# Splitting the row maxima and applying the first norm on GpSimd, and a router chain of one step per slot, in a fused memory, attention and expert kernel

## The reference, cut to what matters

```python
z = layernorm(x)                       # "the first norm" of this text
q, k, v = z @ Wq + bq, z @ Wk + bk, z @ Wv + bv
probs = softmax(einsum("bqhd,bkhd->bhqk", q, k) / sqrt(8))
attn = einsum("bhqk,bkhd->bqhd", probs, v) @ Wo + bo
x2 = layer_norm(z + attn) * ln1_g + ln1_b
keys = x2 @ router_w + router_b
expert = floor(keys) mod 4
out = x + layer_norm(x2 + expert_ffn[expert](x2)) * ln2_g + ln2_b
```

## Time and profile before

| | |
|---|---|
| median of 3 runs | 1465.96 us (1462.61 to 1480.37) |
| the profiled execution | 1456.27 us, span 1454.5 us |
| busy over the span | PE 1163.3 us (80%), DVE 1035.3 (71%), ACT 790.5 (54%), POOL 490.2 (34%) |
| maxima reduced on VectorE, L1287 | 1024 times, 643.0 us busy |
| exponentials on ScalarE, L1012 | 1024 times, 548.5 us busy |
| mean granted TensorE clock | 0.889 of full speed |

### The profile page before, as it was taken

The page is one execution under the profiler, slowest core; times in us unless marked ns, Lnnn a source line. Parts: engine busy times, 40 slices in busy tenths (PEclk is TensorE's granted clock), DMA queues, the critical chain, the costliest instruction groups (busy, mean ns, idle before and its releaser), DMA issues. The chain is left out here.

```text
span 1454.5 us, 24976 instructions
## 1 busy us (share of the span) xinstructions
PE 1163.3 (80%) x6087; PEld 464.3 (32%) x6087; DVE 1035.3 (71%) x2549; ACT 790.5 (54%) x1638; POOL 490.2 (34%) x579
## 2 busy tenths in 40 slices
PE   4978894479889889889889889889889850887872
PEld 4754452112223323323323323323322210333331
DVE  7357772578889889889989889889889321355553
ACT  2323331027677677677767678678677740443431
POOL 6323333011043143143143243243242231245453
PEclk9998875559899999999989899899999985999996
DMA  5000000422332332332331431431431004344340
GB/s 140 3 1 0 0 0 0 87 66 49 64 82 46 83 82 44 83 82 44 82 82 37 89 82 34 92 82 32 94 81 25 16 15 149 116 122 139 111 145 6
DMA packets 101868, 94.12 MB, mean 65 GB/s; under 512 B 23101, under 2 KB 93182, under 8 KB 101768
## 3 DMA queue, kind: packets, MB, share of 16 engines
q1 hardware_dynamic: 94968, 80.19, 23.5%
q0 software_dynamic: 5504, 12.73, 2.7%
q10 hardware_dynamic: 1296, 0.20, 0.1%
HBM read 50.83 MB, written 42.92 MB: 64 GB/s over the span
## 5 line engine op out<-in xcount | busy, mean ns | idle before, releaser
L1287 DVE TENSOR_REDUCE a_mx<-ps_x 128x1 f32<-128x512 f32 x1024 | 643.0, 682 | 108.0 <-PE ps_x L938 100.9
L1012 ACT ACTIVATE a_prob<-ps_s 128x512 f32<-128x512 f32 x1024 | 548.5, 598 | 197.2 <-PE ps_s L945 184.4
L938 PE MATMUL ps_x<-ks,a_qs 48*128 48x512 bf16 x1024 | 291.6, 415 | 106.4 <-DVE a_mx L1287 63.7
L960 PE MATMUL ps_o<-a_prob,vaug 128*32 128x512 f32 x2048 | 287.4, 634 | 0.2 <-ACT a_prob L1012 0.2
L945 PE MATMUL ps_s<-a_qs,ks 50*128 50x512 bf16 x1024 | 245.2, 398 | 6.8 <-ACT a_prob L1012 6.6
L938 PEld LDWEIGHTS ps_x<-ks,a_qs 48*128 48x128 bf16 x1024 | 70.8, 94 | 447.4 <-DVE a_mx L1287 297.5
L1139 POOL DMA_INDIRECT rows<-a_row,a_pos_i x64 | 64.4, 1006 | 154.3 <-DVE a_pos_i L1262 132.1
L1417 POOL DMA_INDIRECT out<-e_result,e_ids x76 | 75.0, 986 | 98.1 <-DVE e_result L1593 76.5
L1078 POOL TENSOR_TENSOR a_rstd<-a_vareps,a_neghalf 128x4 f32<-128x4 f32 x16 | 16.6, 1038 | 240.5 <-DVE a_vareps L1197 240.5
L945 PEld LDWEIGHTS ps_s<-a_qs,ks 50*128 50x128 bf16 x1024 | 76.5, 95 | 44.1 <-ACT a_prob L1012 31.3
L1471 PE MATMUL ps_f<-e_x_t,e_w 128*128 128x512 f32 x152 | 71.9, 617 | 8.9 <-DMA e_biases<-biases_all 8.9
(11 more groups left out here) (213 smaller groups left out, 1555.9 us busy)
## 6 DMA issues: line engine op xcount, KB each, us to landing
stacks<-a_parts SPq DMA_DIRECT2D x192, 128.0 KB, 2.4
a_qs<-stacks SPq DMA_DIRECT2D x64, 192.0 KB, 4.7
ks<-stacks SPq DMA_DIRECT2D x64, 192.0 KB, 5.1
e_rows<-rows SPq DMA_DIRECT2D x19, 520.0 KB, 3.8
e_w<-in_L_ffn_W SPq DMA_DIRECT2D x38, 256.0 KB, 3.9
rows<-e_padding SPq DMA_DIRECT2D x7, 520.0 KB, 3.1
out<-e_result,e_ids POOLq DMA_INDIRECT x76, 3.4
maxima<-a_mparts SPq DMA_DIRECT2D x64, 8.0 KB, 1.4
```

Of the source, the lines that this page charges most:

```text
L938: pe.matmul(ps_x[:, n % BANKS, :], qs[1 - r][own, pair, qt * P:(qt + 1) * P], ks[1 - r][own, pair, :], start=True, stop=True).then_inc(mx_ ...
L960: mm = pe.matmul(ps_o[32 * j:32 * j + VW, :], vaug[r][:, kt, 4 * g + j, :], prob[:, v % RING, j, :], start=(v == first), stop=(v == last))
L1012: act.activation(prob[:, (s // 2) % RING, u % 4, :], ps_s[:, u % BANKS, :], ACT.Exp, scale=SCALE).then_inc(exp_done, EXP_STEP)
L1287: dve.tensor_reduce(mx[:, half, col:col + 1], ps_x[:, n % BANKS, :], AX.X, ALU.max)\
```

## The change

The maxima are split by GpSimd in SBUF ahead of their transpose. The transpose is then one bf16 product with 64 rows out, and ScalarE copies it out of `ps_m`. GpSimd also computes `z`, by a subtraction and a multiplication over all four tiles, with the reciprocal root between them. The routing chain has one operation in most slots from slot 25 on, and its second half moves to slots 3 to 6 of the next step, as `rk` (now bf16, five passes) moves to slot 1 and the scatter behind the first norm; so there is one more step. The parts of q and k are spilled each as soon as it is there. `MISC` has new slots, and GpSimd's list a new order. Cut to its core:

```diff
-    MISC = (("mx1", 1, 0), ("vg", 3, 2), ("v", 4, 1), ("ob", 5, -1), ("at", 7, -1), ("z", 9, 2), ("wo", 11, -1),
-            ("q", 13, 2), ("k", 15, 2), ("mx0", 19, 1), ("rk", 27, -1), ("oa", 29, 0))
-    MIDDLE = 18
+    MISC = (("rk", 1, -2), ("vg", 3, 2), ("v", 4, 1), ("ob", 5, -1), ("mx1", 6, 0), ("at", 8, -1), ("z", 11, 2),
+            ("wo", 13, -1), ("q", 15, 2), ("k", 17, 2), ("mx0", 21, 1), ("oa", 29, 0))
+    MIDDLE = 20
-    FIRST, LAST = -2, B
+    FIRST, LAST = -2, B + 1
+    ROUTE = 25
...
 SyncE
-                if on(i, 0):
-                    wait(sp, misc_free, used(i, "mx1"))
-                    spill_maxima(1)
                 if on(i, 1):
                     wait(sp, spilled, SPILLS * (i + 2))
                     wait(sp, qk_mm, i * UNITS)
                     stack(1 - r, 1, st1_in)
                 if on(i, 0):
+                    wait(sp, misc_free, used(i, "mx1"))
+                    spill_maxima(1)
                     shift(i, r, 1, sh1_in)
                 if on(i, 2):
+                    wait(sp, misc_free, used(i, "k"))
+                    spill(i + 2, r, 0)
+                    wait(sp, middle_done, i + 3)
+                    spill(i + 2, r, 1)
                     wait(sp, split_step, 2 * (i + 3))
-                    spill(i + 2, r)
+                    spill(i + 2, r, 2)
...
 TensorE
-                    mm = pe.transpose(ps_m[0:H // 2 * T, 0:P], mx[:, half, :], ident[:])
+                    mm = pe.matmul(ps_m[0:2 * SHIFTS * PAIRS // 2 * T, 0:P], mx_parts[:, half]..., ident_b[:], ...)
...
 ScalarE
+                    for half, name, d in ((1, "mx1", 0), (0, "mx0", 1)):
+                        if s == slot_of(name) and on(i, d):
+                            act.wait_ge(misc_full, used(i, name))
+                            wait(act, (sh0_in, sh1_in)[half], SHIFTED * (i + d))
+                            act.activation(mparts[:, half, :], ps_m[0:2 * SHIFTS * PAIRS // 2 * T, 0:P], ACT.Copy)\
+                               .then_inc(misc_free, 1)
...
 GpSimd
+            def split_maxima(b, half):
+                wait(pool, max_done, UNITS * b + (UNITS if half else UNITS // 2))
+                wait(pool, misc_full, used(b - 2 + half, ("mx0", "mx1")[half]))
+                whole = mx[:, half, :].rearrange("p (h m) -> p h m", h=2)
+                pool.tensor_copy(mx_parts[:, half, :, 0, :], whole).then_inc(msplit_step, 1)
+                pool.wait_ge(msplit_step, 2 * (2 * b + half) + 1)
+                pool.tensor_tensor(mx_parts[:, half, :, 1, :], whole, mx_parts[:, half, :, 0, :], ALU.subtract)\
+                    .then_inc(msplit_step, 1)
...
+                if on(i, 0):
+                    split_maxima(i, 1)
                 (copy of vg_t)
+                    wait(pool, mean_done, T * (i + 3))
+                    pool.tensor_scalar(vareps[:], mv[:, :, 1], EPS, 1.0, ALU.add, ALU.mult).then_inc(vareps_done, 1)
+                    pool.tensor_tensor(z[:], x_tok[:, tokens(i + 2), :], spread(mv[:, :, 0]), ALU.subtract)
                     pool.tensor_tensor(rstd[:], vareps[:], neghalf[:], ALU.pow).then_inc(rstd_done, 1)
+                    pool.tensor_tensor(z[:], z[:], spread(rstd[:]), ALU.mult).then_inc(z_done, 1)
+                if on(i, -2):
+                    scatter(i - 2)
                 (zb; second norm: vareps2, shift2, rstd2, tnorm)
+                (copies of the residual and the number into row)
+                if on(i, 1):
+                    split_maxima(i + 1, 0)
                 (first subtraction for q and k)
+                (tnorm * ln_g)
                 (second subtraction for q and k)
-                (copies into row; tnorm * ln_g)
                 (+ ln_b, router product, number)
-                (scatter of sequence i - 1)
...
 VectorE
-                    if s == 2 and on(i, 0):
-                        split_maxima(i, 1, r, used(i, "mx1"))
-                        dve.tensor_scalar(vareps[:], mv[:, :, 1], EPS, None, ALU.add).then_inc(vareps_done, 1)
-                    if s in (8, 9) and on(i, 2):
-                            dve.tensor_scalar(z[:, t:t + 1, :], x_tok[:, tile_of(i + 2, t), :], mv[:, t, 0:1], rstd[:, t:t + 1],
-                                              ALU.subtract, ALU.mult).then_inc(z_done, 1)
-                    if s == 20 and on(i, 1):
-                        split_maxima(i + 1, 0, 1 - r, used(i, "mx0"))
-                    if s == 25 and on(i, -1):        # five operations
-                    if s == 26 and on(i, -1):        # two
-                    if s == 28 and on(i, -1):        # five
+                    if s == ROUTE and on(i, -1):     # waits for kprod_done; then one in each of the slots to ROUTE + 6
+                    if s == slot_of("rk") + 2 and on(i, -2):    # slot 3: place and count, which frees ps_m
+                    ...                                          # slots 4, 5 and 6: one operation each
```

More of the change, by code:

```diff
@@ L832, in spill_maxima @@
             def spill_maxima(half):
-                own = PAIRS // 2 * T
+                own = SHIFTS * PAIRS // 2 * T
                 for hh in range(2):
-                    sp.dma_start(maxima[half, hh].rearrange("n m t -> m n t"), mparts[own * hh:own * (hh + 1), half])\
+                    sp.dma_start(maxima[half, hh].rearrange("n m t -> (n m) t"), mparts[own * hh:own * (hh + 1), half, :])\
                       .then_inc(mspilled[half], 16)
@@ L891, in misc @@
                 elif name == "z":
[L892 removed]
+                    wait(pe, z_done, 2 * (i + 3))
                     for n, t in enumerate(tiles):
@@ L902, in misc @@
                     half = int(name[2])
-                    wait(pe, max_done, UNITS * (i + 1) if half else UNITS * (i + 1) + UNITS // 2)
-                    mm = pe.transpose(ps_m[0:H // 2 * T, 0:P], mx[:, half, :], ident[:])
+                    wait(pe, msplit_step, 2 * (2 * i + 2) if half else 2 * (2 * i + 3))
+                    mm = pe.matmul(ps_m[0:2 * SHIFTS * PAIRS // 2 * T, 0:P], mx_parts[:, half].rearrange("p h n m -> p (h n m)"),
+                                   ident_b[:], start=True, stop=True)
                 elif name[0] == "o":
```

137 lines of the change are left out of this document (78 added, 59 removed).

## The result

The changed kernel took 1428.3 us (median of four executions), the kernel before 1468.3 us beside it: a ratio of 0.971, 95% interval 0.963 to 0.980. Two later sets gave 0.972 (0.965 to 0.979) and 0.980 (0.974 to 0.987). Executions more than 1.5% longer than the fastest of their kernel are left out of every ratio but not of the medians, so a ratio here is not always the quotient of the two medians beside it. The changed kernel is faster by 2 to 3% (the interval of the third set alone would also allow 1.3%), and the forecast of 1436 us lay 8 us from the median. The account behind it was much less right than the total: the gain does not lie where I had put it.

A forecast was written before the change was run, and what follows sets the result against it. VectorE and TensorE were taken to bound the attention steps in turns. Steady state -22, SyncE -2 and fill -6 gave -30 us, from a median of 1466 to 1436 us; range 1395 to 1470, the forecast's own 1422 to 1452.

The forecast's parts named there:

- z, 1.0 us of VectorE a step: First norm moved to GpSimd: two pieces, each holding back VectorE's next reduction by 0.50 us, saved; hidden on GpSimd.
- The split of the maxima, 1.0 us: Split taken off VectorE: 0.51 us saved twice a step.
- z's transpose in slots 10 to 17, +0.4: It shares these slots with three projections, where TensorE bounds: 0.4 us a step lost.
- The path to the router's product: GpSimd, from the second norm's statistics: 13.4 us, so VectorE waits 1.1 us at slot 25; ScalarE waits 0.75 us.
- The routing chain, 1.1 us: VectorE's chain from slot 25, spread to single operations costing 0.1 us each: 2.9 us becomes 1.85, saving 1.1 a step.
- The clock, left as it was: Low clock costs up to 31 us, some 18 behind the routing chain; taken as unchanged, pause 1.7 against 1.47 us.
- The steady state, -22 us: Net of -1.6 us a step over 14 steps, from VectorE's -3.2, the wait's +1.1 and the transpose's +0.4.
- The fill, -6 us: Earlier spill: step -2 gains 5.6 less 1.8 for z on GpSimd; the wait of 5.13 us shrinks by 2.
- SyncE in the steady state, -2: Spill ending about 5.6 us sooner trims the wait at a step's first slot by 0.3 us in half the steps.
- rival 2: Nothing comes of it: VectorE's slot pairs stay as long, only the fill is gained; 1460 us, 18%.
- rival 1: Router's product in time at slot 25: 15 us more gained, and 18 us of low clock; 1403 us, 25%.
- rival 3: GpSimd becomes the bound, slowed by a quarter beside VectorE: wait of 4.5 us at slot 25; 1502 us, 12%.

The follow-up runs named there:

- Experiment 12: Changed kernel with the first norm applied on VectorE again, in two pieces in slots 9 and 10: 1430.9 us beside 1432.3 for the changed kernel.
- Experiment 7: Changed kernel with all twelve spill DMAs again behind the last subtraction: 1499.5 us, ratio 1.041 to the kernel before.
- experiment 8: Changed kernel with GpSimd's router product ahead of the second subtraction and the output row copies: 1416.3 us beside 1451.8 for the kernel before.
- Experiment 4: Changed kernel with GpSimd's two copies into the output row behind its first subtraction for q and k, no longer ahead: 1431.1 us.
- experiment 11: Changed kernel with the routing chain drawn together again, five operations in slot 25, two in slot 26, four in slot 3: 1453.9 us.
- experiment 6: Kernel before with only the spill of q and k in parts, each as it becomes ready: 1446.7 against 1451.8 us, ratio 1.001.
- experiments 2: Changed kernel with GpSimd's four scatter DMAs one operation later, behind the addition of the output bias: 1429.0 us.
- experiment 10: Changed kernel with the router's product first and the attention output's transpose in slot 9, not 8: 1425.5 us against 1432.3 for the changed kernel.

## Why the prediction came out right, and where it was wrong

The total (1436 forecast, 1428 to 1436 measured in three sets) and the direction were right. That the total is so close is in good part luck. The traces give 21 us for the forecast's 30, with 8 where it had 24 (the steady state) and 12 where it had 6 (the fill), and the medians' difference is closer to 40 by some 20 us that no trace shows. By its own steps:

- **z, 1.0 us of VectorE a step: wrong.** The step that failed is the measure itself, "by how long it holds back the reduction behind it". The insertion did hold back one reduction by 0.50 us, but TensorE's products for slot 9 come late behind the attention output's transposes, and VectorE got most of the time back as idle time there. Experiment 12 has the price in the changed kernel: 0.3 us.
- **The split of the maxima, 1.0 us: as forecast where it stood.** The slots that held it went from 1.7 to 1.2 us, twice a step.
- **z's transpose in slots 10 to 17, +0.4: too small.** Slots 4 to 15 lost 0.9 us net although VectorE had less to do there. Two stalls of 0.8 and 1.1 us came. The second is the whole loss: in experiments 7 and 8, which don't have it, the same slots took 20.2 us. The forecast looked at where z went and not at the transpose of the attention output, which the same table moved from an odd slot into an even one behind the value products, nor at the scatter, which came from the end of the step into this stretch.
- **The path to the router's product: right.** 13.5 us against 13.4, ScalarE's wait 0.77 against 0.7. The wait of VectorE at slot 25 was 0.26 and not 1.1 us, because the same late subtraction had stopped it at slot 23 already. Experiment 4 moved the loss from there to slot 25 with no gain, and experiment 8 took it away: 1.0 us a step in slots 16 to 24, as the forecast priced it, of which 0.4 to 0.5 came back behind slot 24.
- **The routing chain, 1.1 us: about right** (0.9 in experiment 11).
- **The clock, left as it was: wrong.** Slots 25 to 31 lost most of their low clock, 1.5 us a step, close to the 18 us over twelve steps that the forecast had put behind the chain. Slots 0 to 3 got 0.6 us of it back. The 0.9 us that remain, with 0.8 from VectorE's lighter chain, pay for the new stalls. The forecast set the gain to nothing, since a pause of 1.7 us would stay at slot 25; TensorE's wait there was 1.52 us before and is 0.98 now. That the shorter wait is what keeps the clock up is not shown: with 1.6 to 2.2 us in experiment 11 it stayed up in six steps of ten. The forecast also read the low clock of rows 7 as the consequence of that wait, which half of the steps with the same wait don't bear out.
- **The steady state, -22 us: wrong**, since it is the sum of these. The traces show 2 us over eleven steps, with the two steps at its edges 6 more.
- **The fill, -6 us: half of the true size.** It was 12, as in the kernel with the spill alone (experiment 6). Step -2 came out nearly as forecast: with the spill alone it gained 5.8 us (forecast 5.6), and with z on GpSimd 4.3, so z took off 1.5 us (forecast 1.8; an operation took 1.04 us and not 1.28). The term that failed is the other one, a wait shorter by 2 for the two steps behind it: they gained 4.3 and 3.3 us. That each makes the same chain of spills and loads with little to hide it fits this.
- **SyncE in the steady state, -2: right for the order of the kernel before, wrong for the new one.** With the spill alone the loop took 600.3 us instead of 602.2. Experiment 7 shows that the new order needs it: without the parts each step takes 3.5 us more.
- **Rivals.** Nothing came of it for VectorE in the steady state, or nearly so, as rival 2 has it, and the low clock behind the chain mostly vanished, as rival 1 has it, though the product was not in time; GpSimd never became the bound in rival 3's sense, its first subtraction staying at 2.14 us. TensorE had no wait for `ps_m` in slots 3 or 6.
- **Steps of 52.3 us and the first product of step 0 at 315 us:** the steps took 54.6 us on average, and the product came 77.9 us after the addition of the residual instead of 86.3, so at 313 us on the scale of the first profile.

What stays open: the stall of 1.0 us at slot 12. Of the eleven traces of the changed kernel and its variants nine have it in slot 12 or 13, in nearly every step. It moved with the scatter in two (experiments 2 and 12) and was absent in two in which the scatter had not moved (7 and 8). TensorE's signals, from z's transposes on, are late where it is in slot 12. Why they are is not known. The changed kernel has it in all three of its traces, but each variant has a single trace, so its absence in two may as well be a draw of the execution as a result of the edit. Open, too, is what moves the low clock, and up to 20 us of the medians' difference of 40, which are in executions without a trace.

The shortest loop of all traces is that of experiment 8, 580.9 us. Its median (1416.3) was not taken beside the unaltered changed kernel, and the trace is one execution, so by how much it beats it is an estimate: from the rests, 7 to 13 us. About 12 us of the loop's 20 are the missing stall, so it isn't shown that the edit would bring all of this again; the same edit in experiment 10 had the stall and a rest of 1196.3 us, as the changed kernel.

## What to carry to other kernels

Work taken off an engine gives time back only where that engine bounds the whole stretch: holding back the next instruction is not yet a price, so ask what the neighbour would have been waiting for anyway. When a table of slots is shifted to make room for one piece, look at every other piece that it moves, its parity and what shares its slot. And before two traces are compared, cut each at the first instruction of the part that was changed; here half of the first pair's difference lay ahead of it. Last, follow the low clock through the whole step before a gain is put down to it: here it left one stretch and turned up in the next.

## What the runs showed of the hardware

- The same code in the same place drew one of two paces: the gather stage's f32 transposes took 272 ns in the median in two executions, one of each kernel, in which the attention began at 215 us, and 421 ns in the twelve others with a trace, in which it began at 224 to 236 us. In two of those twelve (experiments 4 and 6) the clock's record covers this stretch, and it has the 1.2 GHz level from 38 to 89 us; in the other ten the record begins behind it. In a program of one core that is more than most edits here were worth.
- One small operation in a slot of its own holds VectorE back by about 0.1 us (slots 25 to 27 took 1.27 to 1.37 us with one, 1.21 without); four in a row behind the sum cost 0.9 us.
- A wait of TensorE of 1.52 us, in the same place in 22 steps of two executions, was followed within 3 us by a stretch at the 1.2 GHz level in eleven of them and not in the others.
- Two of GpSimd's broadcast operations of 128x512 for z took 1.04 us each, against 1.26 to 1.28 for those with a row of parameters repeated for each tile, although the number of elements is the same.
